# Two layers of attention and mixture of experts: the first attention's beginning, the first mixture's order and the cut of five-tile score rows

## What is computed

```
x = x + L0_attn(layernorm(x))   # layernorm with scale and bias, 16 heads of width 8, softmax(q k^T / sqrt(128)) v, plus the normalised input
x = x + L0_ffn(layernorm(x))    # 8 experts, the best 2 by sigmoid(x @ gate_W), hidden width 64, gelu, and a shared expert
x = x + L1_attn(layernorm(x))   # rope, 8 query heads on 4 key/value heads of width 128, causal softmax, Wo
x = x + L1_ffn(layernorm(x))    # rms norm, 16 experts, the best 4 by softmax, swiglu, residual
```

## Time and profile before

| | us |
|---|---|
| median of 3 timed runs | 982.95 (982.52 to 983.34) |
| the profiled execution | 979.61 |
| its span, first to last instruction | 977.5 |
| TensorE busy | 900.5 (92%) |
| VectorE busy | 729.1 (75%) |
| ScalarE busy | 620.4 (63%) |
| GpSimd busy | 360.5 (37%) |

### The profile page before, as it was taken

The page is one execution under the profiler, slowest core; times in us unless marked ns, Lnnn a source line. Parts: engine busy times, 40 slices in busy tenths (PEclk is TensorE's granted clock), DMA queues, the critical chain, the costliest instruction groups (busy, mean ns, idle before and its releaser), DMA issues.

```text
span 977.5 us, 17521 instructions
## 1 busy us (share of the span) xinstructions
PE 900.5 (92%) x6208; PEld 583.6 (60%) x6208; DVE 729.1 (75%) x1499; ACT 620.4 (63%) x1251; POOL 360.5 (37%) x401
## 2 busy tenths in 40 slices
PE   3689999999999999979699999999999999898998
PEld 1312223222222322535588889888988899787897
DVE  7789999999999998648655554655455547797877
ACT  3268888888888888534755555555555554365665
POOL 5700000000000010221676769396929683246422
PEclk9779999999999999989899999999999999999999
DMA  2410111110000000000000000000000012000000
GB/s 67 140 51 24 42 42 39 45 44 19 25 22 18 18 2 18 1 0 18 1 1 1 1 17 1 2 11 7 1 1 2 1 34 55 1 2 12 11 13 12
DMA packets 23374, 20.10 MB, mean 21 GB/s; under 512 B 5176, under 2 KB 17440, under 8 KB 23288
## 3 DMA queue, kind: packets, MB, share of 16 engines
q1 hardware_dynamic: 23288, 18.99, 6.6%
HBM read 14.26 MB, written 4.59 MB: 19 GB/s over the span
## 4 chain that ended last, share of the span: by engine, by line
PE 62%; DVE 20%; POOL 8%; issue 4%; ACT 2%; DMA 2%; SPq 1%; DVEq 0%; POOLq 0%; ACTq 0%
DVE halves L831 13%; PE a_sum L2182 8%; PE summed L1045 7%; PE m_down L2438 6%; PE score_bank L1032 5%; PE a_turn L2167 4%; PE max_bank L992 4%; PE max_bank L1005 3%; PE a_scores L1700 3%; PE a_scores L1701 3%; PE a_scores L1702 3%; POOL a_crossed L1780 2%; POOL a_rotated L1782 2%; PE m_hid L2256 1%; PE m_hid L2257 1%
## 5 line engine op out<-in xcount | busy, mean ns | idle before, releaser
L956 ACT ACTIVATE probs<-score_bank 128x512 f32<-128x512 f32 x512 | 267.6, 602 | 74.7 <-PE score_bank L1032 74.5
L831 DVE TENSOR_REDUCE halves<-max_bank 128x2 f32<-128x1024 f32 x256 | 298.6, 1219 | 11.8 <-PE max_bank L992 9.7
L1715 ACT ACTIVATE a_probs<-a_scores,a_lowest 128x896 f32<-128x896 f32 (+7 forms) x128 | 94.8, 741 | 113.7 <-DVE a_lowest L1710 112.9
L2182 PE MATMUL a_sum<-a_v,a_turned 128*128 128x128 f32 x1152 | 164.6, 280 | 2.4 <-ACT a_turned L2042 1.5
L2182 PEld LDWEIGHTS a_sum<-a_v,a_turned 128*128 128x128 f32 x1152 | 145.0, 193 | 3.5 <-ACT a_turned L2042 2.1
L992 PE MATMUL max_bank<-k_stack,q_stack 48*128 48x512 bf16 x512 | 117.9, 398 | 25.2 <-DVE halves L831 24.3
L1045 PE MATMUL summed<-probs,v_tile 128*32 128x512 f32 x1024 | 138.7, 614 | 0.0
L1032 PE MATMUL score_bank<-q_stack,k_stack 50*128 50x512 bf16 x512 | 132.5, 385 | 3.6 <-ACT probs L956 2.2
L1710 DVE TENSOR_REDUCE a_lowest<-a_scores 128x1 f32<-128x896 f32 (+7 forms) x128 | 96.2, 755 | 34.1 <-PE a_scores L1704 32.8
L754 POOL COPY v_tile<-values 128x128 f32<-128x128 f32 x16 | 4.6, 293 | 303.9 <-PE summed L1045 303.7
L992 PEld LDWEIGHTS max_bank<-k_stack,q_stack 48*128 48x128 bf16 x512 | 25.3, 94 | 124.0 <-DVE halves L831 109.9
(11 more groups left out here) (343 smaller groups left out, 1630.7 us busy)
## 6 DMA issues: line engine op xcount, KB each, us to landing
rope<-in_rope SPq DMA_DIRECT2D x8, 256.0 KB, 3.1
rope<-in_L_ffn_mlp_w SPq DMA_DIRECT2D x8, 256.0 KB, 4.8
q_parts<-l_q_parts SPq DMA_DIRECT2D x2, 768.0 KB, 4.9
k_parts<-l_k_parts SPq DMA_DIRECT2D x2, 768.0 KB, 6.4
q_stack<-q_parts SPq DMA_DIRECT2D x30, 48.0 KB
k_stack<-k_parts SPq DMA_DIRECT2D x30, 48.0 KB
x<-in_L_attn_x SPq DMA_DIRECT2D x2, 512.0 KB, 4.2
q_stack<-shift SPq DMA_DIRECT2D x64, 2.0 KB
```

The lines of the kernel that those rows point to most:

```text
L831: dve.reduce_max(halves[:, u % 2, half, :].rearrange("p (x t) -> p x t", x=2)[:, :, qt], max_bank[place % RING][:, :, :], AX_X).then_inc(f ...
L956: act.activation(probs[:, step % PROBS, x, :], score_bank[e % SCORES][:, :], ACT.Exp, scale=SCALE0).then_inc(prob_ready, 1)
L1715: act.activation(probs[:, k % 2, c, 0:row_width(n)], scores[n % 2][:, 0:row_width(n)], ACT.Exp, bias=lowest[:, n % 8:n % 8 + 1], accum_out ...
L2182: last_use = pe.matmul(sum_bank[:, c * P:(c + 1) * P], turned[:, m % SLOTS, i * P:(i + 1) * P], v[:, b, first + i, q, :], start=(first + i ...
```

## The change

1. *First attention, low parts.* VectorE makes the low parts of the first batch element's keys (units 2 and 3; semaphore `first_k_lo`), GpSimd the six others. VectorE's four first rests stand together, before the two later normalise chunks. Rests 6 and 7 stand inside the ring, ahead of the searches 1 and 2.
2. *First attention, loads.* The first pair's query stack is loaded by ScalarE, after the queries' own send (`first_q_out`); SP loads the key stack and waits until both are there before it sends the parts of all heads.
3. *First attention, values.* ScalarE copies the values; TensorE's value products stand in the ring, one chunk before each of the searches 2 to 5.
4. *First mixture.* Chunks 0 and 1 are written out. The second gate has a place of its own (`routing_bank`, beside the parts), its first half stands before chunk 1's spreads and its second before chunk 1's first expert sum; the shared product of chunk 2 stands behind chunk 1's third sum; ScalarE scores before chunk 2's activations; VectorE weighs chunk 1's third product before the ranking and the fourth between ranking and marking. GpSimd splits the chunks 2 and 3 after the parts' copies of both first chunks.
5. *Second attention.* A row of five tiles starts at column 128 of its two banks, so that its pieces are 384 and 256 columns wide instead of 512 and 128.

```diff
+        def low(engine, i):
+            which, c, cols = unit(i)
+            engine.wait_ge(mid_ready, i + 1)
+            return engine.tensor_tensor(parts[which][:, 2, cols], rest[:, i % 4, :], parts[which][:, 1, cols], ALU.subtract)
...
+        def load_first(engine, stack, which):
+            for x in range(2):
+                rows, head = slice(x * ROW, x * ROW + NST), slice(x * HD0, (x + 1) * HD0)
+                engine.dma_start(stack[rows, :], first_dram[which][:, head, :]).then_inc(loaded[0], 16)
...
-                sp.wait_ge(lo_ready, (which + 1) * CB)
+                sp.wait_ge((lo_ready, first_k_lo)[which], CB)
...
-            sp.wait_ge(first_out, 16 * 6)
-            load_first()
+            sp.wait_ge(first_out, 16 * 3)
+            load_first(sp, k_stack[0], 1)
+            sp.wait_ge(loaded[0], loads_by(0))
             send_parts(0)
...
-            for i in range(2 * NCH):
-                which, c, cols = unit(i)
-                pool.wait_ge(mid_ready, i + 1)
-                pool.tensor_tensor(parts[which][:, 2, cols], rest[:, i % 4, :], parts[which][:, 1, cols],
-                                   ALU.subtract).then_inc(lo_ready, 1)
+            for i in (0, 1, 4, 5, 6, 7):
+                low(pool, i).then_inc(lo_ready, 1)
...
             find(1)
-            take_rest(0)
-            take_rest(1)
+            for i in range(4):
+                take_rest(i)
+            for i in range(2, 4):
+                low(dve, i).then_inc(first_k_lo, 1)
             normalise_chunk(2)
-            take_rest(2)
-            take_rest(3)
             normalise_chunk(3)
-            for i in range(4, 8):
-                take_rest(i)
-            for c in range(NCH):
-                take_values(c)
+            take_rest(4)
+            take_rest(5)
             for use in ring_uses():
+                if use in (("search", 1), ("search", 2)):
+                    take_rest(5 + use[1])
...
             mid(3)
+            act.wait_ge(first_q_out, 16 * 3)
+            load_first(act, q_stack[0], 0)
             take_turned(2)
...
             mid(7)
+            for c in range(NCH):
+                take_values(c)
...
-            for c in range(NCH):
-                project_values(c)
             pe.wait_ge(rest_ready, 4)
             for event in ring_before():
+                if event[1] in range(RING, RING + NCH) and event[0] == "search":
+                    project_values(event[1] - RING)
                 give_ring(event)
...
-        part_bank = ps("m0_part", [3 * E0, CH], BF16)
+        routing_bank = ps("m0_routing", [P, CH])
+        part_bank, gate_bank = routing_bank[0:3 * E0, 0:CH // 2].bitcast(BF16), routing_bank[:, CH // 2:CH // 2 + TB * E0]
...
-            weigh_hidden(1, 0)
-            weigh_hidden(1, 1)
+            for m in range(3):
+                weigh_hidden(1, m)
             dve.wait_ge(prob_ready, 1)
             m0.rank(dve, chain, 1)
-            weigh_hidden(1, 2)
+            weigh_hidden(1, 3)
             m0.mark(dve, chain, 1)
-            weigh_hidden(1, 3)
             m0.weigh(dve, chain, 1).then_inc(parts_ready, 1)
...
             take_turned(FIRST + 1)
+            act.wait_ge(gate_ready, 2)
+            m0.score(act, gate_bank, 1).then_inc(prob_ready, 1)
             for j in range(3):
                 activate(act, 2, j)
-            act.wait_ge(gate_ready, 2)
-            m0.score(act, spare, 1).then_inc(prob_ready, 1)
+            leave(1)
             for j in range(3, NU):
                 activate(act, 2, j)
-            leave(1)
...
+            turn_in(FIRST + 1)
+            gate(0)
+
+            first_weights(1)
+            sum_shared(1)
+            gate(1)
+            sum_expert(1, 0)
+            spread_weights(1, 2)
+            pe.wait_ge(done.freed, done.last_place + 1)
+            turn_sum(0)
+            sum_expert(1, 1)
+            spread_weights(1, 3)
+            up(pe, 2, 0)
+            sum_expert(1, 2)
+            up(pe, 2, 1)
+            sum_expert(1, 3)
+            for j in range(2, NU):
+                up(pe, 2, j)
+            pe.wait_ge(parts_ready, 1)
+            turn_parts(2)
+            up(pe, 3, 0)
...
+        def row_start(n):
+
+            return P if row_width(n) == CH + P else 0
```

More of the change, by code:

```diff
@@ L653, in send_first @@
                         src = parts[1][0:2 * HD0, 0:copies, 0:S]
[L654 removed]
+                    sp.dma_start(first_dram[which][done:done + copies, :, :].rearrange("a r s -> r a s"), src).then_inc((first_q_out, first_out)[which], 16)
                     done += copies
[L657 to L661 removed]
             def send_parts(b):
                 for which in range(2):
[L665 removed]
+                    if b == 0 and which == 1:
+                        sp.wait_ge(first_k_lo, CB)
+                    else:
+                        sp.wait_ge(lo_ready, (b + which + 1) * CB)
                     sp.dma_start(t.parts_dram[which][:, b * P:(b + 1) * P, :].rearrange("a r s -> r a s"),
@@ L1695, in score @@
             tile = half * QB + c
[L1696 to L1699 removed]
+            width, at = (tile + 1) * P, row_start(n)
+            for first, cols in row_pieces(n):
+                dst, rows = scores[n % 2][:, at + first:at + first + cols], slice(tile * P, (tile + 1) * P)
                 pe.matmul(dst, qT[0][:, b, q, rows], kT[0][:, b, first:first + cols], start=True, stop=False)
```

133 lines of the change are left out of this document (67 added, 66 removed).

## The result

The changed kernel takes 972.17 us (median of 4 executions, 971.64 to 972.92), the kernel before on the same chip 983.14 (982.52 to 983.68): ratio 0.9889, interval 0.9872 to 0.9906. The forecast was 972.0 us, range 966.5 to 977.0. In a later comparison the same two kernels stood at 972.83 and 982.39, ratio 0.9909 (0.9892 to 0.9926); ratios are of all executions, not of the two medians. Executions of one kernel spread: the kernel before took 977.1 to 985.6 us in all that were timed in this study, and its profiled one, 979.61, is one of the better ones. So the two profiled spans differ by 7.4 us (977.5 and 970.1), the medians by 9.6 to 11.0.

A forecast was written before the change was run, and what follows sets the result against it. VectorE and TensorE bound the first attention, TensorE the second; transfers chain the start, and TensorE idles in the mixture. Start -2.0, mixture -7.4, rows -1.5 sum to -10.9 us: 968.7 from the profile, median 972.0, range 966.5 to 977.0.

The forecast's parts named there:

- The mixture: First mixture: the new order ends TensorE's waits and the half clock after them; -7.4 us, bounds -8 and -4.
- Rival 2: First mixture: TensorE stands some 3 us before chunk 3's parts, ScalarE reloading its table late; -7.2 us in all, 975.8; 15%.
- The five-tile rows: Second attention: 384 + 256 columns save 0.10 us in each of 16 rows; -1.5 us, bounds 0 and -2.5.
- rival 4: Second attention: narrow pieces cost nothing, the second piece's time is its columns'; -9.4 us in all, 973.5; 10%.
- The start: First attention's beginning: earlier low parts, loads and SP queue bring searches and first score forward; -2.0 us, bounds -5.5 and +1.5.
- GpSimd's three operations: Start: GpSimd's long operations come some 4 us later, covered before the first score; without cover, 2 us.
- the rests in the ring: Start: two rests inside the ring cost VectorE 1.3 us, leaving 1.7 us of the 3.0 us search gain.
- SP's queue: Start: SP sends the parts from 28.7 instead of 30.8, so the first score moves by 2.1 us.
- rival 1: Start gives nothing: ScalarE's wait delays the projections and SP's queue is no earlier; -8.9 us in all, 974.0; 17%.
- the 3.3 us: Whole kernel: the profiled execution, 979.6, lay 3.3 us under the timed median 982.95, so 968.7 became 972.0.
- Rival 5: Slower: stretches at 1.2 GHz grow in the first attention after its first score; 985.6 after 85 us more; 3%.
- Rival 3: Start gives its full bound: value products keep TensorE's clock up through the searches; -14.4 us in all, 968.5; 13%.

The follow-up runs named there:

- alone: Only the first mixture's new order put into the kernel before: 975.17 us beside 981.68, ratio 0.9929 (0.9912 to 0.9946).
- score later: Changed kernel, but ScalarE scores the second gate behind two activations of chunk 2, not ahead of them: 978.98 us, ratio 0.9964 to the kernel before.

## Why the prediction was right, and where it was not

The number was right (972.0 against 972.17); of the three terms behind it two held and one failed, so that the number comes that near is luck.

*The mixture: right, step by step.* Forecast -7.4; in the trace -7.6, alone -7.0 (-8.6 to -5.3). The exponential was expected near 419 (419.29), the ranking from 420.6 (421.23), the parts ready near 426.8 (427.8), asked for near 427.4 (428.04). They are 0.3 to 1.0 us later, of which 0.6 is the first attention's. The parts were ready 0.2 us before TensorE asked for them, so the slack just held and nothing new was waited for. The same stretch is 7.6 us shorter in every profile with this order, score later apart. Rival 2, ScalarE's table reload in the way, didn't come: the reload stands at 419.53, over 2 us before the next activation.

*The five-tile rows: right.* -1.5 forecast as 16 x 0.10; each row is 0.10 us shorter, and the stretch -0.7 to -2.0 between the same events, by the traces and not by the times. The Trainium skill ("TensorE: Matmul & The Clock Gate", back-to-back issue gap) has the isolated gap go with the columns plus 2.5 ns, by which both cuts cost the same; rival 4 was the same view, and the rows speak against it. The same section says that this formula counts too little for narrow products that each load weights, about 81 ns at 128 columns; the trace agrees in direction, with 0.28 us for three (0.09 each on average). The prediction did not use that sentence. Why a narrow f32 product is dear was not tried by an experiment.

*The start: the step that failed.* Forecast -2.0 (first search at 31.5, first score at 50.1, first attention 1.7 to 2.1 us shorter). The first half came nearly as told: low parts ended at 20.93 (21.5), keys asked for at 25.13 (25.8). Then came four things.

First, the two loads on ScalarE's queue took 2.05 us and SP's 1.71, so the third chunk's copy came at 25.53 (25.2), the projections at 26.36 (26.0), and the last of them ended at 32.66; the first search came 1.1 us later than forecast. Only 0.4 of it is the later start: the projections took 6.3 us at a granted clock of 0.58, where before they took 4.6 at 0.79 (25.52 to 30.07).

Second, the prediction wrote of GpSimd's three operations that they come later, "covered, since nobody uses them before the first score". Nobody uses their result, but they hold VectorE's joining: 1.65 us for 0.17 (0.66 in the other profiles with the old start), on the chain. The price of VectorE beside GpSimd had been looked up for the low parts alone, where it hardly came due (1.47 for two against 1.28). The Trainium skill ("GPSIMD Engine Reference", its table) says that the two contend when VectorE has two SBUF inputs; the joining has two, and the trace agrees to the end time, 45.05 against 45.03, while the reductions, which read PSUM, keep 1.15 us each beside it.

Third, the rests in the ring were priced right (1.3 us), but with a gain of 1.9 at the first search in place of 3.0 they left 0.7 in place of 1.7, and the joining took that and more. Fourth, the forecast took the first score to move with SP's queue, 2.1 us. The queue came 2.9 us earlier and the score 0.3, since the shift itself was written 0.8 us later: the wait had passed from the transfer to VectorE.

So rival 1, to which I gave 17%, is what happened by its outcome: the start gives nothing, though SP's queue was earlier, which it denied. Its total, -8.9 us, is what the second comparison measured (0.91% of 982.39), and the first one's interval (-9.2 to -12.6) holds my -10.9 and nearly that.

*What carried the number nonetheless.* Luck. From profile to profile the change gives 7.7 us (979.61 to 971.92), not the forecast's 10.9; the 3.3 us that were added for the kernel before's good profile have no counterpart in the changed kernel, whose profile and median lie 0.3 apart. As the median of the kernel before the forecast's 982.95 was well taken (981.7 to 983.1 in four of its five comparisons), but the start's missing 2 us are within what one comparison of 4 executions leaves open: the second comparison gives 8.9 to 9.6 us, the first 10.9.

*Slower, and the clock.* Rival 5 had no part in it: from 52 to 62 us the clock stood at 0.50 (0.52 before), and from 62 to 65 it was up again at 0.94. Rival 3, the start's full bound, failed with the first search: TensorE's clock did stay up longer, 0.64 in place of 0.50 in 37.8 to 52.24, but VectorE was the bound there.

## What to carry to other kernels

When a long operation of GpSimd is moved, look not at who needs its result but at what VectorE does meanwhile: its small instructions with two SBUF inputs are held, and one of them on the chain costs the whole rest of GpSimd's operation. They aren't the only ones: four normalise instructions, with one tensor as input, took 2.79 us beside GpSimd's low parts and eight of them 2.13 us where GpSimd stood idle (changed kernel, from 20.85). A second DMA queue is only free if the engine that owns it has nothing behind the wait; here the idle SP gave more than ScalarE. And a one-off result that closes a loop over three engines (gate, exponential, ranking, sum) goes ahead of all that only feeds throughput: without that one position 7 of the 10 us were gone.

## What the runs showed of the hardware

- A joining of 128 x 8 elements takes 0.17 us, and 1.65, 0.92 or 0.66 us where it meets GpSimd's operation of 128 x 2048; it ends when that ends.
- In f32 score rows three products of 128 columns start 0.05 and 0.12 us apart and the mask 0.11 behind the last; products of 256 columns start 0.12 apart. The second piece's three products take 0.28 us at 128 columns, 0.36 at 256 (559.76 to 560.12) and 0.53 at 384. The first of these in the kernel before, the last in the changed one, both TensorE's timeline:

```profile
567.04 0.22 PE L1700 MATMUL a_scores<-a_kT,m_room 128*128 128x128 f32 x1
567.09 0.28 PE L1701 MATMUL a_scores<-a_kT,m_room 128*128 128x128 f32 x1
567.21 0.27 PE L1702 MATMUL a_scores<-a_kT,m_room 128*128 128x128 f32 x1
```

The changed kernel:

```profile
564.94 0.34 PE L1743 MATMUL a_scores<-a_kT,m_room 128*128 128x384 f32 x1
...
565.47 0.23 PE L1747 MATMUL a_scores<-a_mask,a_identity 128*128 128x128 bf16 x1
```

- Two loads of the same size took 2.05 us to issue on ScalarE's queue beside SP's sends and loads; SP alone took 1.71 and 1.45 for such pairs.
- A profile's total of this kernel moves by 1.6 us with one stretch of low clock that comes or not at the same code, so two profiled spans don't measure a change of 1%; the start times of one instruction in the same loop, just behind the changed place, do.
